# Cross-attention and stream-mixing kernel: six Sinkhorn groups for five, and mixing tiles taken from one queue

## The reference, cut to what matters

```python
x = x + xattn(layernorm(x), ctx, ctx)        # softmax(q) * SCALE, softmax(k), context = k v^T, out = context q, Wo, norm over rows
x = x + ffn(layernorm(x))

# ffn, for each token with its 4 streams of 512 columns:
H_res  = sinkhorn(logits_res)                # 4x4 per token, 50 rounds of row and column normalisation, tau = 0.1
H_pre, H_post = softmax(logits_pre), softmax(logits_post)
y      = (sum_n H_pre[n] * x_streams[n]) @ W_branch
out[i] = sum_j H_res'[i, j] * x_streams[j] + H_post[i] * y
```

## Time and profile before

| | |
|---|---|
| median of the runs | 3085.62 us |
| profiled execution, its own time | 3098.09 us |
| its span | 3096.3 us |
| TensorE busy | 2768.3 us (89%) |
| VectorE busy | 1707.6 us (55%) |
| ScalarE busy | 984.6 us (32%) |
| GpSimd busy | 819.3 us (26%) |
| mean granted TensorE clock | 0.943 |
| L662, mixing products | 219.6 us busy, 178.7 us idle before, most of it until mix_w |

### The profile page before, as it was taken

How to read it: one execution, slowest core, us unless ns; L and a number is a source line. 1 busy time by engine, 2 the same in 40 slices (tenths; PEclk the granted TensorE clock), 3 DMA queues, 4 the chain that set the end, 5 groups by cost and what they waited for, 6 DMA issues and landing times.

```text
span 3096.3 us, 34900 instructions
## 1 busy us (share of the span) xinstructions
PE 2768.3 (89%) x12024; PEld 1873.9 (61%) x12024; DVE 1707.6 (55%) x4279; ACT 984.6 (32%) x2311; POOL 819.3 (26%) x685
## 2 busy tenths in 40 slices
PE   8999999989899899999989899998988998967943
PEld 5766666666666566666656666665665665634610
DVE  2444545365767734356675745445677652487454
ACT  1333333332323223243323333333233332422411
POOL 2322323240313224132321214233132331320400
PEclk9999999999999999999989999998999999979965
DMA  7112120303021132413114132411413134211333
GB/s 235 35 64 80 36 101 31 112 28 116 28 89 41 62 94 62 142 56 118 59 45 137 56 112 64 148 58 59 141 57 123 46 99 151 87 50 34 99 94 88
DMA packets 203064, 258.22 MB, mean 83 GB/s; under 512 B 45320, under 2 KB 111496, under 8 KB 202888
## 3 DMA queue, kind: packets, MB, share of 16 engines
q1 hardware_dynamic: 202888, 255.99, 26.1%
HBM read 180.04 MB, written 75.89 MB: 83 GB/s over the span
## 4 chain that ended last, share of the span: by engine, by line
PE 76%; DVE 14%; issue 4%; DMA 2%; ACT 2%; POOL 1%; SPq 1%; DVEq 0%; POOLq 0%; ACTq 0%
PE big L600 15%; PE kc_bank L543 13%; PE big L575 13%; PE big L518 11%; PE tb L662 4%; PE tb L651 4%; PE tb L585 4%; PE tb L529 3%; PE misc L617 3%; PE misc L630 3%; PE kc_bank L614 2%; DVE stats L781 1%; DVE skw L967 1%; DVE skr L968 1%; DVE ska L965 1%
## 5 line engine op out<-in xcount | busy, mean ns | idle before, releaser
L1128 ACT COPY turned<-tb 128x512 f32<-128x512 f32 x512 | 298.4, 586 | 1087.2 <-PE tb L585 638.8
L518 PE MATMUL big<-ctx_sb,wk 128*128 128x512 f32 x1024 | 513.6, 629 | 28.9 <-ACT k_exp L1119 28.9
L600 PE MATMUL big<-merged,turned 128*128 128x256 f32 x2048 | 496.6, 385 | 25.2 <-ACT turned L1128 25.0
L543 PE MATMUL kc_bank<-ctxt,turned 128*128 128x256 f32 x2048 | 493.3, 387 | 8.8 <-ACT turned L1128 8.8
L575 PE MATMUL big<-wqs,x_sb 128*128 128x512 f32 x1024 | 490.6, 605 | 2.5 <-DVE q_sb L860 1.9
L600 PEld LDWEIGHTS big<-merged,turned 128*128 128x128 f32 x2048 | 377.7, 190 | 134.9 <-issue 54.1
L543 PEld LDWEIGHTS kc_bank<-ctxt,turned 128*128 128x128 f32 x2048 | 383.8, 195 | 74.0 <-issue 29.4
L1338 POOL TENSOR_TENSOR qhalf<-q_sb 128x512 f32<-128x512 f32 x128 | 162.5, 1270 | 900.5 <-ACT q_sb L1133 900.4
L662 PE MATMUL tb<-mix_ld,mix_w 121*96 121x512 f32 (+1 forms) x344 | 219.6, 731 | 178.7 <-POOL mix_w L1328 130.8
L518 PEld LDWEIGHTS big<-ctx_sb,wk 128*128 128x128 f32 x1024 | 192.8, 201 | 210.9 <-issue 164.6
L1346 POOL TENSOR_TENSOR q_sb<-q_sb,qsum 128x1024 f32<-128x1024 f32 x128 | 243.6, 1903 | 274.7 <-DVE qsum L872 274.7
(11 more groups left out here) (129 smaller groups left out, 3529.3 us busy)
## 6 DMA issues: line engine op xcount, KB each, us to landing
mix_ld<-streams SPq DMA_DIRECT2D x168, 240.0 KB
ctx_sb<-in_ctx SPq DMA_DIRECT2D x64, 512.0 KB, 10.1
ctxt<-in_ctx_t SPq DMA_DIRECT2D x64, 512.0 KB, 4.9
x_sb<-in_x SPq DMA_DIRECT2D x64, 512.0 KB, 9.6
x_tr<-in_x_t SPq DMA_DIRECT2D x64, 512.0 KB, 9.7
streams<-x_sb SPq DMA_DIRECT2D x64, 512.0 KB, 3.1
out<-mix_out SPq DMA_DIRECT2D x168, 192.0 KB, 2.2
streams<-y_sb SPq DMA_DIRECT2D x32, 256.0 KB, 2.0
```

The lines of the kernel that those rows point to most:

```text
L518: t = nc.tensor.matmul(big[i], wk[:, ct, dt * P:(dt + 1) * P], ctx_sb[b % 2][:, ct, quarter(i)], start=ct == 0, stop=ct == CT - 1)
L543: t = nc.tensor.matmul(kc_bank[:, 0:C], turned[n % 3][:, j * P:(j + 1) * P], ctxt[:, nt, :], start=nt == 0, stop=nt == NT - 1)
L600: t = nc.tensor.matmul(big[2 + p % 2][:, half], turned[n % 3][:, dt * P:(dt + 1) * P], merged[:, dt, :], start=dt == 0, stop=dt == DT - 1)
L1128: nc.scalar.copy(turned[k % 3][:], tb[n % 2][:]).then_inc(s_tba, 1)
```

## The change

The group of three batches becomes a group of two and one of one, so there are six groups and six Sinkhorns. Each of the last two iterations then holds a whole Sinkhorn, of two batches in iteration 14 and of one in 15, over all of its places. Steps end one place earlier than before, and tiles are no longer spread evenly over the time to the next end: they come from one queue in order, one at every place whose number in the whole list divides by four, or, while there are many left for the places that remain, at every second place.

```diff
-GROUPS = (4, 4, 4, 3, 1)
+GROUPS = (4, 4, 4, 2, 1, 1)
...
-    ends = [starts[gr] + (starts[gr + 1] - starts[gr]) * 3 // 5 for gr in range(len(GROUPS) - 1)]
+    ends = [starts[gr] + (starts[gr + 1] - starts[gr]) * (3 if GROUPS[gr] > 2 else 5) // 5 - 1 for gr in range(len(GROUPS) - 1)]
...
         put(order_of_places[ends[gr]], "coefs", gr)
-        last = ends[gr + 1] if gr + 2 < len(GROUPS) else len(order_of_places)
-        some = order_of_places[ends[gr] + 3:last]
-        spread(mixes[gr][:len(some)], some)
-        left = mixes[gr][len(some):]
+
+    ready, waiting = [(end + 3, tiles) for end, tiles in zip(ends, mixes)], []
+    for at in range(ends[0], len(order_of_places)):
+        while ready and ready[0][0] <= at:
+            waiting += ready.pop(0)[1]
+        behind = len(waiting) + sum(len(tiles) for _, tiles in ready)
+        if waiting and (at % 4 == 0 or at % 2 == 0 and 4 * behind > len(order_of_places) - at):
+            put(order_of_places[at], *waiting.pop(0))
+    left = waiting + [task for _, tiles in ready for task in tiles]
```

## The result

The changed kernel takes 3177.35 us (3175.64 to 3181.69, 4 runs) against 3085.90 beside it (3084.87 to 3088.16): ratio on record 1.0277, 95% interval 1.0255 to 1.0299. The two medians themselves stand 91 us apart, a ratio of 1.0296, which lies in the same interval. I had forecast 3130 and a range up to 3164: the direction was right, the size about twice what I had worked out. Compared profile to profile, the span grew from 3096.3 to 3180.0, by 83.7 where the sum said 43.9.

What follows compares the result with a forecast made beforehand. The prediction took TensorE as the bound, so the change could move only what makes it wait. Its stage terms summed to +43.9 us on the median 3085.6, giving 3129.5, forecast 3130; own range 3100 to 3152, whole range 3064 to 3164.

Steps and rivals of the forecast that it cites:

- The tile rates: Each mixing tile costs 1.3 us in an iteration's query stage (Q) and 1.0 in its key stage (K).
- Rival 3: Tiles cost 1.0 us in query stages too, and two stages come out low: +4 us, 3090, chance 0.08.
- rival 1: Faster: iteration 15's jam was the one real loss, tiles cost about 0.9 us: -25 us, 3061, chance 0.22.
- The wait behind the twelve loads: Near key place 25 of iterations 7, 11, 13 and 14, TensorE waits 8.6 us, in 14 9.9 us.
- K6 and K10: Key stages of iterations 6 and 10: +1 us for one tile, and +2 us, between -2 and +6.
- 8 and 9, 12, K14 and 15: Iterations 8 and 9 together -21.2 us, 12 +5.8, the key stage of 14 +14.3, iteration 15 -38.6.
- K14's 97.6: Key stage of iteration 14: 83.3 us plus one tile, 2.5 of wait and 49 steps at 0.22: 97.6, +14.3.
- The gain of iteration 15: VectorE's key-stage work falls from 101.1 to 55 us: key stage -29.6 us, query stage -9.
- ten steps +3.2: Key stage of iteration 13: ten more Sinkhorn steps add 3.2 us, in a stage put at 87.7, +5.6.
- rival 2: Slower: VectorE jams in iterations 14 and 12, 15 and 10 us more; 15 gives back only 25: 3165, chance 0.12.
- VectorE 48.4 + 58 x 0.65 + 9 x 0.51 = 91: Query stage of iteration 14: VectorE's work of 91 us, so the stage takes some 118, +1.
- The half-clock term: After each wait behind the loads TensorE runs at half clock, an estimated 3.4 us per wait.

Runs made afterwards that it cites:

- run 7: Changed kernel with the next iteration's twelve loads issued three each at key places 20, 23, 26 and 29 instead of all at 20: 3121.32 us, ratio 1.009.
- run 8: Kernel before the change, its fourth group's steps spread over all of iteration 15, leaving 43 tiles to the tail for 24: 3064.05 us, ratio 0.9918.
- run 5: Changed kernel with the third group's steps over 80 places for 67, its tiles 13 places later: 3149.65 us, ratio 1.0182.
- run 4: Changed kernel with the third group's steps packed closer to end seven places earlier, its tiles left in place: 3183.9 us, ratio 1.0285.
- run 13: Changed kernel with the third group's steps four places later at the same density, coefficients and first tile later too: 3172.6 us, ratio 1.0258.
- Run 3: Changed kernel with the first tile of the two-batch group nine places later: 3179.67 us, ratio 1.0272.
- run 14: The kernel of run 11 with the third group's steps four places later: 3094.21 us, ratio 1.0003.
- run 11: Changed kernel with both the third group's steps over 80 places and the loads spread three at a time: 3103.57 us, ratio 1.002.

## Why the prediction was right and wrong

**The tile rates, right.** 1.3 us a tile in Q and 1.0 in K gave Q6 116.9, Q7 110.4, Q10 116.9, Q11 110.4; measured 115.2, 106.9, 116.3, 108.5, so 1.2 to 1.3 a tile and 1.0 to 1.1. Rival 3, cheap tiles, was half right in this and fell as a whole, and rival 1 with it.

**The wait behind the twelve loads, right** in place, and run 7 shows its cause. The waits themselves were 0.2 to 3.7 us shorter than I had put them. But the burst was worth more than I gave it, 56 us of 3177, since the same queue also held back the first tiles of a group in K6 and K10, which I had left at +1 and +2 and which came out +2.0 and +6.9.

**8 and 9, 12, K14 and 15, right** to 6 us each. K14's 97.6 to the tenth is luck: its wait behind the loads was 6.19 us for the 9.9 in its sum, so the 49 steps and the rest cost some 3.7 more than I gave them. The gain of iteration 15 is the 44 us that I had put at 39, and run 8 shows that the new groups were not needed for half of it.

**Iteration 13, the step that failed.** I wrote for K13 "ten steps +3.2": 0.32 us a step, a rate from iterations 4 and 5, where 97 steps stand over two whole iterations. So the sum had TensorE waiting for nothing but tiles there. Built on the 83.3 us of K14, it gave 87.7; the runs showed 118.0, with 17.64 us of waiting for ScalarE's copy that the sum had at nothing, and products that took 86.0 us at a clock of 0.81 for the 76.0 of K14 at 0.96, with three tiles fewer. In this iteration the steps come seven to every four places, onto the places where VectorE has its statistics, `x_pre` and the key maxima, and ten places take it 35.9 us for 24.8. (Only the steps from place 8 on count as K13's; those of places 0 to 7 are in Q12, and what they delayed shows in K13.) The table shows what that cost: at the same density a later phase, a later centring or half the elements leave the sum between 300 and 310; only 80 places bring it lower (run 5 with 282.9, of whose 34 us some 7 are the seven tiles that moved on). Before's 278.0 held more tiles, 19 for 8, and fewer steps, 92 for 109. The form it took, TensorE waiting for a copy that stood behind ScalarE's logarithm, was one of several (runs 4 and 13 show two more). I had a rule for a jam in rival 2, "once VectorE's work passes some 60 us in a K stage"; K13 had 51 and jammed, K14 had 62 and did not. The measure was wrong: a stage's busy time does not tell what is busy in its first third. (By its own terms that rival's time was 3168, not 3165; and VectorE's steps of four batches took 93.7 us, not 93.8.)

**Q14, the second.** "VectorE 48.4 + 58 x 0.65 + 9 x 0.51 = 91" is the mis-sized term: it was 104.8, or 0.84 for each of the 67 steps. Groups of VectorE's instructions in the kernel after (busy, mean ns of one, idle before): two of Q14, then one of K14 and one of the bare stage Q2:

```profile
L968 DVE TENSOR_TENSOR skw<-skp,skb 128x64 f32<-128x64 f32 x22 | 8.4, 381 | 0.3
L885 DVE TENSOR_SCALAR nrm<-nrm 128x2 f32<-128x2 f32 x8 | 7.8, 981 | 1.5 <-ACT squares L1149 1.5
...
L968 DVE TENSOR_TENSOR skw<-skp,skb 128x64 f32<-128x64 f32 x22 | 4.9, 221 | 0.5
...
L885 DVE TENSOR_SCALAR nrm<-nrm 128x2 f32<-128x2 f32 x8 | 3.5, 440 | 14.5 <-ACT squares L1149 14.5
```

L968 takes 0.38 us where it takes 0.22, on the same shape, and the norm's instruction (L885) 0.98 for 0.44: 3.5 and 4.3 us of the 14. Run 3 shows that VectorE's lateness, and not the way through DRAM, was the 9 to 12 us. The trace shows what made them longer. Only some are: three of L968 took 1.25 to 1.60 us, five of L885 1.23 to 1.55, and all others in the stage 0.10 to 0.28. Each long one began while GpSimd ran L1343 or L1351 and ended just behind it, as here:

```profile
2782.70 1.90 POOL L1351 TENSOR_TENSOR q_sb<-q_sb,qsum 128x1024 f32<-128x1024 f32 x1 [3.15 <-DVE qsum L877]
...
2783.08 1.54 DVE L885 TENSOR_SCALAR nrm<-nrm 128x2 f32<-128x2 f32 x1
```

With those of other lines 14 of VectorE's instructions in Q14 lost 15.0 us in this way, each ending 0.02 to 0.08 us after GpSimd's; in Q14 of before, with 15 steps, it was one, by 0.3 us, and in Q12 of before, with 38, eleven, by 12.4. That is as much as the term was short by. No run took GpSimd's work away from there to see the time come back.

**The half-clock term.** The four waits went with a granted clock of 0.94 in K7 and K11, 0.89 in K14 and 0.81 in K13. TensorE's products in K13 took 13 us more than before, and in run 7 the end of an 8.4 us wait gave K7 11.8. The Trainium skill, "TensorE: Matmul & The Clock Gate", Part 1, says that for modelling the ramp's penalty is below 1% of a typical kernel's span. The trace does not agree with it for a kernel with waits like these: the mean granted clock is 0.936 after and 0.943 before. (The prediction gave 0.88 as the lowest clock of a stage with side work; K15 has 0.87.)

**Left open:** how the 30 us of K13 divide between the steps' density and ScalarE's order. Four places later at the same density took 8.2 us off the three stages in run 13, two tiles among them, and 6.9 in run 14 against run 11. Run 5 took 34, but it moved the logarithms and seven tiles along with the density.

## What to carry to other kernels

Price side work by the densest stretch it will stand in, not by its rate in a sparse one, and look at how long an engine takes for the same few places of its program before and after: its busy share was 94 to 95% in both. Count how much of that side work stands beside another engine's instructions that hold it up. When a wait is moved and the time stays, the engine behind it is late: thin out its work. Ahead of a new grouping, try the two cheap edits first: spread a burst of large loads whose queue also carries small urgent ones, and leave fill-in work to the stretch that another engine's chain sets.

## What the runs showed of the hardware

VectorE's instructions beside GpSimd's centring: L968 took 3.37 us for its usual 0.29, and two of `x_pre` together 4.86 for 0.74 each, while a reduction with one input (L969) took its 0.29. Beside GpSimd's L1343 and L1351, 14 instructions in Q14 took until GpSimd's ended, and 0.02 to 0.08 us more; an L968 begun 0.02 us after an L1343 kept its 0.21. The Trainium skill, "SBUF — State Buffer", SBUF: two separate sides, says that an instruction of VectorE with two SBUF inputs and one of GpSimd exclude each other for the whole instruction. Beside L1343 and L1351 the trace agrees, but L885, which has one input, is held up there too. Beside the centring it agrees on which ones suffer, and not on how long: L968 ended at 2406.67, while GpSimd's instruction, begun at 2402.80, ran 5.45 us, to 2408.25. In K14 an L972 begun 0.3 us into a centring instruction took 3.46 us, and an L968 begun 5.0 us into one took its 0.2. The profile's spans of GpSimd are rough, so the difference can lie in the record.

SyncE's twelve loads took from 1270.6 to 1284.4 to issue in K7, 13.8 us: 0.40 to 0.49 each for the first three, up to 2.12 for those behind. In run 7, with three at a time and three places apart, TensorE waits 0.5 us in all in K7.
